# A graph network's last sweep: block sums accumulated in seven PSUM banks, gathered rows already multiplied by the neighbour weights

## The chip, the cores and the metric

The kernel runs on one core of a Trainium2 chip. The metric is the time of one execution on the device in microseconds (us), the median of several runs. Engines: PE (TensorE, matmuls; PEld are its weight loads), DVE (VectorE), ACT (ScalarE), POOL (GpSimd), SP (SyncE, which here issues DMAs and passes signals on).

## What is computed

12500 nodes with 64 features x, 200000 edges (src, dst) sorted by dst, a vector of 64 per edge. Two layers:

```
h1  = relu(layernorm(x) ...)                        layer 1: attention (GATv2, 4 heads) over
x1  = x + gatv2(h1, src, dst, edge_attr)            the edges of each node, softmax per node
h2  = relu(layernorm(x1) ...)
out = x1 + mean_over_edges_into_n(h2[src]) @ w_l.T + h2 @ w_r.T + b      layer 2
```

The last line is the last sweep: for each node the mean of the rows h2[src] of its edges, times a 64x64 matrix, plus a product of its own row.

## The kernel before, in words

Nodes are cut into 98 blocks of 128, edges into 1563 tiles of 128. Since edges are sorted by dst, the tiles of a block are neighbours; a **slot** is one pair of tile and block (a tile on the border of two blocks has two), padded to 1664, and four slots make a **quad**, so there are 416. The first two stages (up to about 4125 us) sort out layer 1; the columns and lines on them play no part here. Between them and the last sweep the rows h2 are made on DVE in four quarters of the blocks and stored by SP to h2D in DRAM (`stored_rows`, L1312 to L1318).

Then comes a prologue: DVE clears the sums AG (128x6272 in SBUF, L1339) and adds b to X3 (L1352), and PE, ACT and DVE make each pair of blocks' own product: transpose (L1357), copy (L1359), matmul by V_r (L1367), addition to X3 (L1370). Names: BR, ZR, AL, mS, mR, sm are SBUF areas, PS is PSUM, and C is the constant identity.

In the last sweep each engine runs a loop of its own over the quads, and they meet by semaphores:

- POOL (`gathers3`, L1417): one indirect DMA per tile brings its 128 rows h2[src] into a ring of 128 tiles (32 quads) in SBUF. Before each quad it takes one from `gf`, which starts at 7: POOL is at most 7 quads of tiles ahead of DVE's quads of slots (there are more slots than tiles, so the distance grows).
- SP (`landings3`, L1394) turns the landing of a quad into an increment of `landed3`.
- PE (`sums3`, L1441): per slot one matmul of a 128x128 one-hot matrix (which edge goes to which node) by 128 gathered rows, start and stop in one, into one of four PSUM banks (q % 4). It waits for the one-hots (`o3_rdy`, in the order listings p3_1) and for `landed3`; its fourth matmul of a quad increments `a3_rdy` (p3_2).
- DVE (`adds3`): per quad it waits for `a3_rdy`, gives `gf` its increment (L1457), and adds the four 128x64 results into AG (L1460); behind the first of them it makes the one-hots of the quad two further on (`onehots`, L544). `c3_acc` (p3_3) chains the additions.
- ACT (`tables3`, L1379) copies the next column of dst numbers to mR.

Where a matmul reads and an addition writes is loaded into registers from tables (`Table`, L528), for PE from DRAM.

```
                a3_rdy.take(V)
                V.sem_inc(gf.s, 1)
                for k in range(4):
                    c3_acc.take(V)
                    V.tensor_tensor(to[k], to[k], bank3(q)[:, k, :], ALU.add).then_inc(c3_acc.s, 1)
                    if k == 0:
                        onehots(q + 2).then_inc(o3_rdy.s, 1)
```

After a barrier the last phase takes each pair of blocks of AG: transpose (L1484), copy (L1488), matmul by V_l (L1496), times 1/count plus X3 (L1502); SP stores seven pieces of out (L153).

Of the kernel before, what the change touches and what calls it, by code (L numbers as in the profile page):

```python
# [4 lines left out]
NB = 98  # L5
NP = NB * 128
NT = 1563
NS = 1664
# [12 lines left out]
def build(nc, x, src_t, dst_t, dfirst, ea, w_l, b_l, w_r, b_r, w_e, rep, bias, v_l, v_r, cst, trow, out):  # L21
# [67 lines left out]
    h2D = dram("h2D", [NP, F])  # L89
# [4 lines left out]
    tabD = dram("tabD", [3, NS], i32)  # L94
    NQ1 = NS // 4
# [1122 lines left out]
    gf, o3_rdy, a3_rdy, c3_acc, go3, r3f, r3_rdy = flows("p3_", 7)  # L1218
    i3 = flows("i3_", 4)
    S.sem_inc(gf.s, 7)  # L1220
    S.sem_inc(c3_acc.s, 1)
# [7 lines left out]
    bT3 = rbf_[0:1, NS:2 * NS].bitcast(i32)  # L1229
    dma(S, bT3, tabD[0:1, :], dB)  # L1230
# [49 lines left out]
    dH2, h2v = dsem(), h2D.rearrange("(b p) f -> p b f", p=128)  # L1280
# [3 lines left out]
    there = [0] * 4  # L1284

# [26 lines left out]
    def stored_rows(k):  # L1312
# [4 lines left out]
        sv.wait(S)  # L1317
        dma(S, h2v[:, b], H23[:, b], dH2)  # L1318

    normalised_nodes(0)  # L1320
# [7 lines left out]
    stored_rows(0)  # L1328
    variance(1)
    centred(3)  # L1330
    stored_rows(1)
    variance(2)
    variance(3)
    stored_rows(2)
    stored_rows(3)
    sv.wait(Q)
    v(V.tensor_copy(b1_ps, b1))
    v(V.tensor_copy(iota_ps, iota))
    v(V.memset(AG, 0.0))  # L1339
    dB.wait(V)  # L1340
    sg.wait(V)
    dH2.wait(Q)

    sa.wait(A)
    for half in range(4):
        A.copy(mS[:, half, :], sT[:, 16 * half:16 * half + 16]).then_inc(i3[half].s, 16)
        A.copy(mR[:, half, :], rel3[:, 16 * half:16 * half + 16]).then_inc(r3_rdy.s, 1)

    at = {}
    sv.wait(P)  # L1350
    dW.wait(P)
    v(V.tensor_tensor(X3, X3, bc(b1_ps.unsqueeze(1), [128, NB, F]), ALU.add))  # L1352
    for p in range(NB // 2 + 1):
        if p < NB // 2:
            if p >= 2:
                P.wait_ge(sa.s, at["copy", p - 2])
            sp.on(P.transpose(PS[:, p % 2, 0:128], H2[:, 128 * p:128 * p + 128], ident))  # L1357
            sp.wait(A)
            sa.on(A.copy(z4[:, p % 4, :], PS[:, p % 2, 0:128]))  # L1359
            at["copy", p] = sa.n  # L1360
        if p >= 1:
            p -= 1
            P.wait_ge(sa.s, at["copy", p])
            if p >= 4:
                P.wait_ge(sv.s, at["own", p - 4])
            m = PS[:, 2 + p % 4, 0:128].rearrange("p (t f) -> p t f", f=F)
            sp.on(P.matmul(PS[:, 2 + p % 4, 0:128], z4[:, p % 4, :], W3[:, 1, :, :].rearrange("p t f -> p (t f)"),  # L1367
                           start=True, stop=True))
            sp.wait(V)
            sv.on(V.tensor_tensor(X3[:, 2 * p:2 * p + 2, :], X3[:, 2 * p:2 * p + 2, :], m, ALU.add))  # L1370
            at["own", p] = sv.n
    sv.wait(P)

    def tables3():

        with A.Fori(0, NS // 64 - 1) as i:
            for half in range(4):
                r3f.take(A)
                A.copy(mR[:, half, :], rel3[:, ds(i * 64 + 64 + 16 * half, 16)]).then_inc(r3_rdy.s, 1)  # L1379
            close(r3f)  # L1380
        r3f.take(A)
        A.copy(mR[:, 0, :], rel3[:, 0:16]).then_inc(r3_rdy.s, 1)

    landed3, seen = nc.alloc_semaphore("landed3"), Flow("seen")
    S.sem_inc(seen.s, 4)
# [18 lines left out]
    def gathers3():  # L1404

        def some(n):
            for j in range(n):
# [9 lines left out]
                Q.indirect_dma_start(BIG[:, j * F:j * F + F], None, h2D,  # L1417
# [4 lines left out]
        with Q.Fori(0, NG3 // G):  # L1422
            some(G)
        some(NG3 % G)

    def bank3(q):
        return PS[:, q % 4, 0:4 * F].rearrange("p (s f) -> p s f", f=F)

    need = [P.alloc_register(f"nd{q}") for q in range(16)]

    def sums3():

        with P.Fori(0, NS // 64) as i:
            pt = Table(P, tabD[2:3, :], i, "sl", (G - 1) * F, 64)
            P.load(need, needD[0:1, ds(i * 16, 16)])
            for j in range(64):
# [5 lines left out]
                if j % 4 == 3:  # L1442
                    ins.then_inc(a3_rdy.s, 1)
# [99 lines left out]
```

## Time and profile before

| | |
|---|---|
| three runs | 6836.62, 6867.18, 6873.22 us; median 6867.18 |
| span of the profiled execution, first to last instruction | 6810.8 us (the page gives no further time of this execution) |
| busy: PE, DVE, ACT, POOL | 4219.0, 3344.2, 1439.7, 3619.4 us |
| first and last gather of the last sweep | 4417.0 and 6701.6 us |
| moved by DMA | 478 MB, 70 GB/s over the span |

The page divides the span into busy time of each engine and slices; groups of instructions stand by line, with the idle time of the engine just before them and what ended it ("<-remote" is a signal whose sender the trace doesn't name, "<-issue" is no wait at all). Queues that only issue or signal have a q behind the engine's name (DVEq, SPq).

### The profile page before, as it was taken

The page shows a single profiled execution, that of the slowest core. Times are in us where ns is not written, and L with a number is a line of the kernel's source. Part 1 is how long each engine was busy: PE and PEld are TensorE (multiplying, and loading weights), DVE is VectorE, ACT ScalarE, POOL GpSimd, SP SyncE. Part 2 cuts the span into 40 slices and gives each one's busy share as a digit, 9 for nine tenths or more (in the row PEclk, how much of TensorE's full clock was granted, in tenths as well). Part 3 has the DMA queues.
Part 4 walks back from the last instruction along what each step waited for, and adds up shares of the span by engine and source line. Part 5 has one row for each costly group of instructions (what it writes and reads, how often), then busy time and mean ns, then how long its engine had stood idle before and what let it go on. Part 6 is the DMA issues. An engine that isn't in the chain of part 4 may idle for free. (4 is left out here: it accounts for less than half of the span.)

```text
span 6810.8 us, 81310 instructions
## 1 busy us (share of the span) xinstructions
PE 4219.0 (62%) x16760; PEld 3105.7 (46%) x16761; DVE 3344.2 (49%) x8382; ACT 1439.7 (21%) x6145; POOL 3619.4 (53%) x3589
## 2 busy tenths in 40 slices
PE   4777777777777777768999998533333333333335
PEld 3555555555555555644444445333333333333335
DVE  6444444444444444479999998822222222222224
ACT  1111111111111111236666663400000000000000
POOL 2555555555555555305555551056666666666662
PEclk8888888888888888879999998755555555555555
DMA  6333333333333333324343441201111111111111
GB/s 106 92 93 95 93 93 94 95 99 95 96 93 93 98 92 93 98 81 124 110 111 109 110 112 50 57 20 23 23 23 23 23 23 23 23 23 23 23 23 28
DMA packets 609795, 478.35 MB, mean 70 GB/s; under 512 B 424696, under 2 KB 438034, under 8 KB 609334
## 3 DMA queue, kind: packets, MB, share of 16 engines
q1 hardware_dynamic: 440940, 256.05, 14.3%
q0 software_dynamic: 101184, 104.41, 7.2%
q10 hardware_dynamic: 67465, 115.81, 4.7%
q14 instruction: 158, 1.29, 0.1%
q8 instruction: 48, 0.79, 0.0%
HBM read 348.37 MB, written 126.73 MB: 70 GB/s over the span
## 5 line engine op out<-in xcount | busy, mean ns | idle before, releaser
L1417 POOL DMA_INDIRECT BR<-h2D,mS x1564 | 1476.9, 944 | 1007.4 <-issue 451.5
L585 POOL DMA_INDIRECT BR<-hD,AL x1308 | 1247.2, 953 | 1018.4 <-ACT ZR L634 638.4
L1441 PE MATMUL PS<-BR,ZR 128*128 x3328 | 796.1, 426 | 1507.1 <-DVE ZR L544 1086.3
L616 PE MATMUL PS<-Wz,BR 128*128 128x264 f32 x3328 | 1209.0, 449 | 696.3 <-DVE alq L682 319.0
L1441 PEld LDWEIGHTS PS<-BR,ZR 128*128 128x128 f32 x3328 | 735.9, 328 | 1567.3 <-issue 1563.9
L679 DVE SCALAR_TENSOR_TENSOR PS<-PS,a 128x528 f32<-128x528 f32 x832 | 594.8, 715 | 1543.4 <-PE PS L617 653.6
L1460 DVE TENSOR_TENSOR BR<-BR,PS 128x64 f32 x1664 | 362.6, 218 | 1725.3 <-remote 1306.5
L617 PE MATMUL PS<-BR 128*128 x3328 | 1150.8, 431 | 0.0
L940 PE MATMUL PS<-BR,ZR 128*128 128x329 f32 x3328 | 1027.9, 469 | 27.0 <-POOL BR L926 21.0
L616 PEld LDWEIGHTS PS<-Wz,BR 128*128 128x128 f32 x3328 | 653.9, 219 | 839.0 <-issue 587.1
L926 POOL TENSOR_TENSOR BR<-ZR,BR 128x768 f32<-128x768 f32 x416 | 616.1, 1481 | 416.6 <-ACT BR L912 414.7
L954 DVE TENSOR_TENSOR BR<-BR,PS 128x329 f32 x1664 | 812.4, 488 | 20.3 <-PE PS L940 13.2
L617 PEld LDWEIGHTS PS<-BR 128*128 128x128 f32 x3328 | 728.3, 219 | 155.0
L940 PEld LDWEIGHTS PS<-BR,ZR 128*128 128x128 f32 x3328 | 501.4, 188 | 553.3 <-DVE ZR L864 521.1
L642 ACT COPY BR<-PS 128x256 f32<-128x256 f32 x832 | 309.2, 372 | 1917.3 <-PE PS L603 862.0
L682 DVE TENSOR_REDUCE alq<-PS 128x8 f32<-128x528 f32 x832 | 578.3, 698 | 0.0
L1379 ACT COPY mR<-ZR 128x16 f32 x100 | 20.4, 204 | 2243.8 <-issue 1163.6
L864 DVE TENSOR_TENSOR ZR<-PS,mR 128x128 f32<-128x128 f32 x1676 | 473.7, 283 | 2.2 <-PEq L161 2.2
L915 ACT ACTIVATE BR<-ZR,BR 128x64 f32<-128x64 f32 x1664 | 440.8, 336 | 0.0
L634 ACT COPY ZR<-BR 128x64 f32 x1664 | 326.5, 247 | 355.9 <-issue 190.3
L585 POOL DMA_INDIRECT BR<-hD,lmS x256 | 243.4, 951 | 280.6 <-ACT ZR L634 170.7
L603 PE MATMUL PS<-C,ZR 128*128 128x128 f32 x1664 | 342.3, 293 | 69.7 <-ACT ZR L634 44.9
(254 smaller groups left out, 2641.4 us busy)
## 6 DMA issues: line engine op xcount, KB each, us to landing
zD<-ZR ACTq DMA_DIRECT2D x416, 256.0 KB
ZR<-zD SPq DMA_DIRECT2D x416, 256.0 KB, 2.7
BR<-relD SPq DMA_DIRECT2D x105, 512.0 KB
ZR<-ea SPq DMA_DIRECT2D x1664, 32.0 KB
BR<-h2D,mS POOLq DMA_INDIRECT x1564
BR<-hD,AL POOLq DMA_INDIRECT x1308
AL<-hD SPq DMA_DIRECT2D x28, 224.0 KB, 2.6
BR<-hD,lmS POOLq DMA_INDIRECT x256
```

The lines of the kernel that those rows point to most:

```text
L585: Q.indirect_dma_start(HT[:, (t % G) * F:(t % G) * F + F], None, hD, bass.IndirectOffsetOnAxis(at_src, 0)).then_inc(hs[q % 16], 16)
L616: P.matmul(m, zo1[:, p % 2, (j % 2) * 128:(j % 2) * 128 + 128], Wz, start=True, stop=False)
L617: ins = P.matmul(m, ohT[:, (j // 4) % 2, j % 4, :], xr, start=False, stop=True)
L679: return V.scalar_tensor_tensor(m, m, 0.0, bc(a8.unsqueeze(1), [128, 2, MC]), ALU.max, ALU.mult)
L682: return V.tensor_reduce(alq[:, (p // 8) % 2, 8 * (p % 8):8 * (p % 8) + 8].rearrange("p (s h) -> p s h", h=H), scores_of(p).rearrange("p s ...
L864: return V.tensor_tensor(oh[:, (s // 4) % 4, s % 4, :], iota_ps, bc(mR[:, (s // 16) % 4, s % 16:s % 16 + 1], [128, 128]), ALU.is_equal)
L915: ins = A.activation(r[:, n, 192:256], hb[:, k, n, 0, :], ACT.Copy, scale=r[:, n, 259:260])
L926: Q.tensor_tensor(r[:, :, 0:192].rearrange("p s (h f) -> p s h f", f=F), bc(hb[:, q % 4, :, 0, :].unsqueeze(2), [128, 4, 3, F]), bc(r[:, : ...
L940: P.matmul(PS[:, j % 7, 0:AC], oh[:, (j // 4) % 4, j % 4, :], rows2(j // 4)[:, j % 4, :], start=True, stop=True).then_inc(ag_rdy.s, 1)
L954: V.tensor_tensor(a, a, PS[:, j % 7, 0:AC], ALU.add).then_inc(c2_acc.s, 1)
L1417: Q.indirect_dma_start(BIG[:, j * F:j * F + F], None, h2D, bass.IndirectOffsetOnAxis(mS[:, (j // 16) % 4, j % 16:j % 16 + 1], 0)).then_inc ...
L1441: ins = P.matmul(bank3(j // 4)[:, j % 4, :], oh[:, (j // 4) % 4, j % 4, :], rows, start=True, stop=True)
```

## The change

- The rows in DRAM are now g2 = h2 times V_l (`neighbour_rows`): PE transposes a quarter's pairs of blocks in groups of four, ACT copies them to `turned2`, PE multiplies by V_l, ACT copies to YC, and SP stores to g2D. The quarters are 32, 24, 24 and 18 blocks. `turned2` also serves the own products, now 49 matmuls with 13 additions of 128x512.
- PE's matmuls of the sweep accumulate (start and stop False) directly where the block's sum stands: block b in bank (b // 8) % 7. No addition on DVE and no AG.
- ACT (`flush3`): when the slots of eight blocks are through (`placed`), it copies them out, times 1/count, and clears the bank (`flushed`). DVE adds each group of eight to X3 after its one-hots; ACT stores out in pieces of 16 blocks, and the last two blocks go by DVE and SP. The last phase with transposes and matmuls is gone.
- Three increments leave PE per quad: `placed` (to ACT), `gf` (to POOL, no longer by way of DVE), `oh_free` (to DVE, p3_3 in the order listings after).
- Ring of 256 tiles (64 quads), window `gf` of 38 quads, one-hots 16 quads ahead.
- PE waits for `landed3` once in eight slots and for `flushed` once in 16; its tables come from SBUF. Twelve small DVE operations and three small DMAs make the tables.

```diff
-    S.sem_inc(gf.s, 7)
-    S.sem_inc(c3_acc.s, 1)
+    landed3, flushed, placed = (nc.alloc_semaphore(n) for n in ("landed3", "flushed", "placed"))
+    S.sem_inc(gf.s, 38)
+    S.sem_inc(seen.s, 4)
+    S.sem_inc(oh_free.s, 16)
+    S.sem_inc(flushed, 1)
...
-    quarters = [slice(0, 25), slice(25, 49), slice(49, 74), slice(74, NB)]
+    quarters = [slice(0, 32), slice(32, 56), slice(56, 80), slice(80, NB)]
...
+    def neighbour_rows(k):
...
+        def turn(p, n, g):
+            if g >= 2:
+                P.wait_ge(sa.s, at["kept", g - 2])
+            for t in range(n):
+                ins = P.transpose(PS[:, g % 2, 128 * t:128 * t + 128], H2[:, 128 * (p + t):128 * (p + t) + 128], ident)
+            sp.on(ins)
+            sp.wait(A)
+            sa.on(A.copy(turned2[:, 128 * p:128 * (p + n)], PS[:, g % 2, 0:128 * n]))
+            at["kept", g] = sa.n
+
+        def product(p, n, g):
+            P.wait_ge(sa.s, at["kept", g])
...
+            for t in range(n):
+                ins = P.matmul(PS[:, 4 + g % 2, 128 * t:128 * t + 128], turned2[:, 128 * (p + t):128 * (p + t) + 128], V_l,
+                               start=True, stop=True)
+            sp.on(ins)
+            sp.wait(A)
+            sa.on(A.copy(YC[:, 128 * p:128 * (p + n)], PS[:, 4 + g % 2, 0:128 * n]))
...
+        sa.wait(S)
+        dma(S, g2v[:, quarters[k]], YC3[:, quarters[k]], dG2)
...
-    v(V.memset(AG, 0.0))
...
+    RING, ONES, BANKS = 256, 16, 7
+    oh3 = BIG[:, 16384:16384 + ONES * 512].rearrange("p (q s n) -> p q s n", q=ONES, n=128)
...
+    v(V.memset(PS[:, 0:BANKS, :].rearrange("p k c -> p (k c)"), 0.0))
...
-                Q.indirect_dma_start(BIG[:, j * F:j * F + F], None, h2D,
+                Q.indirect_dma_start(BIG[:, j * F:j * F + F], None, g2D,
...
         with P.Fori(0, NS // 64) as i:
-            pt = Table(P, tabD[2:3, :], i, "sl", (G - 1) * F, 64)
-            P.load(need, needD[0:1, ds(i * 16, 16)])
+            row = Table(P, rows_of, i, "sl", (RING - 1) * F, 64)
+            to = Table(P, sums_at, i, "pb", (8 * BANKS - 1) * F, 64)
+            P.load(gate[0:8], need_at[0:1, ds(i * 8, 8)])
+            P.load(gate[8:12], spill_at[0:1, ds(i * 4, 4)])
             for j in range(64):
-                rows = ahead(P, BIG[:, ds(pt(j), F)])
+                if j % 16 == 0:
+                    P.wait_ge(flushed, P.snap(gate[8 + j // 16], min_val=1, max_val=15 - BANKS))
+                rows, sums = ahead(P, BIG[:, ds(row(j), F)]), ahead(P, SUMP[:, ds(to(j), F)])
                 if j % 4 == 0:
                     o3_rdy.take(P)
-                    P.wait_ge(landed3, P.snap(need[j // 4], min_val=1, max_val=NG3 // 4))
-                ins = P.matmul(bank3(j // 4)[:, j % 4, :], oh[:, (j // 4) % 4, j % 4, :], rows, start=True, stop=True)
+                if j % 8 == 0:
+                    P.wait_ge(landed3, P.snap(gate[j // 8], min_val=1, max_val=NG3 // 4))
+                ins = P.matmul(sums, oh3[:, (j // 4) % ONES, j % 4, :], rows, start=False, stop=False,
+                               skip_group_check=True)
+                if j % 4 == 0:
+                    ins.then_inc(placed, 1)
+                if j % 4 == 1:
+                    ins.then_inc(gf.s, 1)
                 if j % 4 == 3:
-                    ins.then_inc(a3_rdy.s, 1)
+                    ins.then_inc(oh_free.s, 1)
...
+            for q in range(16):
+                oh_free.take(V)
+                V.tensor_tensor(oh3[:, q % ONES, :, :], bc(iota_ps.unsqueeze(1), [128, 4, 128]),
+                                bc(rel3[:, ds(i * 64 + 4 * q, 4)].unsqueeze(2), [128, 4, 128]), ALU.is_equal
+                                ).then_inc(o3_rdy.s, 1)
...
+    def flush3(g):
+
+        A.wait_ge(placed, A.snap(ends_r[g], min_val=1, max_val=NS // 4))
+        for u in range(8):
+            b = 8 * g + u
+            ins = A.activation(SUMS[:, b * F:b * F + F], PS[:, g % BANKS, u * F:u * F + F], ACT.Copy, scale=rc[:, b:b + 1])
+        sa.on(ins)
+        sa.wait(A)
+        A.activation(PS[:, g % BANKS, :], nothing, ACT.Copy, scale=0.0).then_inc(flushed, 1)
...
+    def added3(g):
+
+        V.wait_ge(flushed, g + 2)
+        sv.on(V.tensor_tensor(X[:, 512 * g:512 * g + 512], X[:, 512 * g:512 * g + 512], SUMS[:, 512 * g:512 * g + 512], ALU.add))
```

DVE where the sweep begins; before (AG's additions, PS the four banks, BR the sums):

```order
L1452 UNCONDITIONAL_BRANCH [waits p3_6]
L1452 ISA
L528 TENSOR_LOAD BR
L529 ISA
L533 ISA x2
L533 REGISTER_ALU
L1460 TENSOR_TENSOR BR<-BR,PS 128x64 [waits p3_2,p3_3]
L544 TENSOR_TENSOR ZR<-PS,mR 128x512
L1460 TENSOR_TENSOR BR<-BR,PS 128x64 [waits p3_3] x3
```

and after (L1455 clears the seven banks, L1529 is the loop's start):

```order
L1452 TENSOR_TENSOR AL<-AL,PS 128x128 [waits sp]
L1455 MEMSET PS 128x3584 [waits sv]
L1529 UNCONDITIONAL_BRANCH [waits d23,sv]
L1532 ISA [waits p3_3]
L1532 TENSOR_TENSOR BR<-PS,ZR 128x512
```

The four additions with their chain are out of the loop, and what is left per quad is a wait for `oh_free` and one 128x512 operation. DVE behind its loop, after:

```order
L1532 ISA [waits p3_3]
L1532 TENSOR_TENSOR BR<-PS,ZR 128x512
L1529 REGISTER_ALU [waits p3_3]
L1529 COMPARE_AND_BRANCH
L1561 TENSOR_TENSOR AL<-AL,BR 128x512 [waits flushed] x12
L1581 SCALAR_TENSOR_TENSOR AL<-PS,rc,AL 128x64 [waits p3_3]
L1581 SCALAR_TENSOR_TENSOR AL<-PS,rc,AL 128x64
```

Twelve additions of eight blocks stand behind all one-hots, and each waits for ACT's flush; in the kernel before the loop was followed by a barrier and 98 L1502.

PE where the sweep begins; before:

```order
L1433 UNCONDITIONAL_BRANCH [waits sv]
L1435 TENSOR_LOAD needD_ptr
L1435 ISA
L1435 REGISTER_ALU
L1435 TENSOR_LOAD needD
L528 TENSOR_LOAD tabD_ptr
L528 ISA
L528 REGISTER_ALU
L528 TENSOR_LOAD tabD
L529 ISA
L1441 MATMUL PS<-BR,ZR 128x64 [waits p3_1,landed3]
L529 ISA
```

and after (the loads from ZR at L1507 and L1508 are the two gates, L529 the two tables):

```order
L1504 UNCONDITIONAL_BRANCH [waits d26,sv]
L1504 ISA
L1507 TENSOR_LOAD ZR
L1508 ISA
L1508 TENSOR_LOAD ZR
L529 ISA [waits flushed]
L529 TENSOR_LOAD BR
L530 ISA
L529 TENSOR_LOAD ZR
L530 ISA
L1517 MATMUL PS<-BR 128x64 [waits p3_1,landed3]
L530 ISA
```

The loads from DRAM have become loads from SBUF, one more table is read, a wait for `flushed` has come in ahead, and the matmul has no bank of its own.

## Rows read from the trace of the kernel before

**Rows 1.** The page's first line.

```profile
span 6810.8 us, 81310 instructions
```

**Rows 2.** Busy time by stretch: us, busy (xcount) of PE, PEld, DVE, ACT, POOL; PEclk; DMA share; GB/s.

```profile
4417.00:4452.00 35.00, 11.97 (x45) 8.89 (x45) 9.38 (x14) 3.70 (x15) 26.56 (x28) 0.60 0.11 26
...
4484.00:6702.00 2218.00, 739.69 (x3087) 682.52 (x3086) 536.46 (x1927) 19.57 (x96) 1449.64 (x1536) 0.50 0.11 23
6702.00:6781.00 79.00, 54.49 (x234) 51.23 (x234) 42.28 (x153) 1.02 (x5) 0.58 (x1) 0.50 0.01 1
6781.00:6811.00 30.00, 26.05 (x146) 19.03 (x145) 23.29 (x98) 12.99 (x49) 0.00 (x0) 0.90 0.48 108
```

**Rows 3.** The gathers (L1417): durations in ns; idle time ended by, us and times.

```profile
L1417 POOL DMA_INDIRECT BR<-h2D,mS x1564: 939/945/1062, 4417.0 to 6701.6; - x196
...
  issue: 451.5, 1482
  DVEq L1457: 357.3, 81
```

**Rows 4.** Waits in 4480 to 6811: waiting operation, releaser: us, times, longest.

```profile
DVE BR L1460 <- remote: 1306.5, 132, 16.7
```

**Rows 5.** Groups of instructions in 4480 to 6811: busy us, mean ns, idle before.

```profile
L1441 PE MATMUL PS<-BR,ZR 128*128 x3328 | 796.1, 426 | 1507.1 <-DVE ZR L544 1086.3 <-issue 411.3
...
L1460 DVE TENSOR_TENSOR BR<-BR,PS 128x64 f32 x1664 | 362.6, 218 | 1725.3 <-remote 1306.5 <-issue 198.7 <-PE PS L1441 122.5
L544 DVE TENSOR_TENSOR ZR<-PS,mR 128x512 f32<-128x512 f32 x416 | 284.3, 684 | 0.2 <-issue 0.2
```

**Rows 6.** The same view, 6702.7 to 6781.

```profile
L544 DVE TENSOR_TENSOR ZR<-PS,mR 128x512 f32<-128x512 f32 x30 | 20.5, 684 | 0.0
```

**Rows 7.** Timeline, middle of the last sweep: start, duration, operation, idle before it.

```profile
5601.13 3.67 PE L1441 MATMUL PS<-BR,ZR 128*128 x16 [2.09 <-issue]
...
5608.86 1.96 PE L1441 MATMUL PS<-BR,ZR 128*128 x8 [4.06 <-DVE ZR L544]
...
5617.94 0.94 POOL L1417 DMA_INDIRECT BR<-h2D,mS  x1 [0.30 <-issue]
5622.88 0.22 DVE L1460 TENSOR_TENSOR BR<-BR,PS 128x64 f32 x1 [13.52 <-remote]
...
5623.56 0.94 POOL L1417 DMA_INDIRECT BR<-h2D,mS  x1 [4.67 <-DVEq L1457]
...
5639.32 0.22 DVE L1460 TENSOR_TENSOR BR<-BR,PS 128x64 f32 x1 [7.38 <-remote]
```

**Rows 8.** The additions of the stage before (L954), idle time ended by.

```profile
  PE PS L940: 13.2, 21
```

**Rows 9.** Register loads of a table from SBUF on PE (first stage).

```profile
L528 PEldq TENSOR_LOAD <-sm x104: 1102/1107/1297, 165.3 to 2961.4; - x104
```

**Rows 10.** Waits in 4415 to 4484, as rows 4.

```profile
ACT BR L1359 <- remote: 25.2, 6, 6.8
```

**Rows 11.** Timeline before and at the start of the gathers, as rows 7.

```profile
4390.80 1.82 DVE L1316 SCALAR_TENSOR_TENSOR BR<-BR,sm 128x1600 f32<-128x1600 f32 x1
...
4407.19 1.76 DVE L1316 SCALAR_TENSOR_TENSOR BR<-BR,sm 128x1536 f32<-128x1536 f32 x1
...
4416.97 1.06 POOL L1417 DMA_INDIRECT BR<-h2D,mS  x1 [198.67 <-DVE BR L1339]
...
4417.67 0.42 PE L1357 MATMUL PS<-C,BR 128*128 128x128 f32 x1
...
4418.31 0.42 PE L1357 MATMUL PS<-C,BR 128*128 128x128 f32 x1
```

**Rows 12.** Timelines of the end, and landing time of the stores (L153).

```profile
6706.11 3.48 PEld L1441 LDWEIGHTS PS<-BR,ZR 128*128 128x128 f32 x16 [2.25 <-SPq L1394]
...
6807.75 0.37 SPq L153 DMA_DIRECT2D out<-AL  x1
...
DMA to landing us min/median/max: 3.0/3.0/3.5
```

More of the change, by code:

```diff
@@ L94, in build @@
     tabD = dram("tabD", [3, NS], i32)
+    tab3D = dram("tab3D", [3, NS], i32)
     NQ1 = NS // 4
@@ L1228, in build @@
             dma(S, W3[64 * t:64 * t + 64, w, t, :], frm, dW)
-    bT3 = rbf_[0:1, NS:2 * NS].bitcast(i32)
-    dma(S, bT3, tabD[0:1, :], dB)
+    from3 = sm[:, 11, 0:26].rearrange("p (t k) -> p t k", t=2).bitcast(i32)
+    with nc.allow_non_contiguous_dma(reason="two small tables, once"):
+        for t in range(2):
+            dma(S, from3[:, t, :], tabD[t, :].rearrange("(k p) -> p k", p=128), dB)
     dma(S, X3, x.rearrange("(b p) f -> p b f", p=128), dX)
@@ L1372, in build @@
[L1372 to L1385, printed above, removed]
+    RING, ONES, BANKS = 256, 16, 7
+    oh3 = BIG[:, 16384:16384 + ONES * 512].rearrange("p (q s n) -> p q s n", q=ONES, n=128)
@@ new lines, in build @@
+    v(V.tensor_copy(grp, to3[:, 2, :]))
+    v(V.tensor_scalar(grp, grp, float(2 - BANKS), 1.0, ALU.add, ALU.max))
+    v(V.tensor_copy(to3[:, 2, :], grp))
+    sv.wait(A)
+    with nc.allow_non_contiguous_dma(reason="three small tables, once"):
+        for t in range(3):
+            dma(A, tab3D[t, :].rearrange("(k p) -> p k", p=128), to3[:, t, :], dT3)
+    v(V.tensor_tensor(below3, bc(blk.unsqueeze(1), [128, 12, 13]), bc(iota[:, 8:104:8].unsqueeze(2), [128, 12, 13]), ALU.is_lt))
+    sv.wait(P)
@@ new lines, in build @@
+    sp.on(P.matmul(PS[:, 6, 0:156], allone, below3.rearrange("p g k -> p (g k)"), start=True, stop=True))
+    sp.wait(V)
+    v(V.tensor_reduce(ends, PS[:, 6, 0:156].rearrange("p (g k) -> p g k", k=13), AX.X, ALU.add))
+    v(V.tensor_scalar(ends, ends, 6.0, None, ALU.add))
+    v(V.tensor_copy(ends_i, ends))
+    v(V.tensor_scalar(ends_i, ends_i, 2, None, ALU.arith_shift_right))
+    sums_end = sv.n
+    dT3.wait(A)
+    dTL = dsem()
+    dma(A, rows_of, tab3D[0:1, :], dTL)
+    dma(A, sums_at, tab3D[1:2, :], dTL)
@@ new lines, in build @@
+    with nc.allow_non_contiguous_dma(reason="each eighth and each sixteenth entry of two small tables"):
+        dma(A, need_at, needD[0:1, 1:NQ1:2], dTL)
+        dma(A, spill_at, tab3D[2:3, 15:NS:16], dTL)
+    v(V.tensor_copy(b1_ps, b1))
+    v(V.tensor_copy(iota_ps, iota))
+    v(V.tensor_tensor(X3, X3, bc(b1_ps.unsqueeze(1), [128, NB, F]), ALU.add))
+    P.wait_ge(sa.s, at["stored", group[0] - 1])
+    for g in range(13):
+        p, n = 4 * g, min(4, NB // 2 - 4 * g)
+        if g >= 6:
+            P.wait_ge(sv.s, at["own", g - 6])
+        for t in range(n):
+            ins = P.matmul(PS[:, g % 6, 128 * t:128 * t + 128], turned2[:, 128 * (p + t):128 * (p + t) + 128], V_r,
+                           start=True, stop=True)
+        sp.on(ins)
+        sp.wait(V)
+        sv.on(V.tensor_tensor(X[:, 128 * p:128 * (p + n)], X[:, 128 * p:128 * (p + n)], PS[:, g % 6, 0:128 * n], ALU.add))
+        at["own", g] = sv.n
@@ L1387, in landings3 @@
+    sv.wait(V)
+    v(V.memset(PS[:, 0:BANKS, :].rearrange("p k c -> p (k c)"), 0.0))
+    sv.wait(P, A)
+    dTL.wait(P)
+    dR.wait(V)
     def landings3():
```

176 lines of the change are left out of this document (82 added, 94 removed).

## The prediction

> **What bounds the kernel now.** I read the page first for its slices, then the windows of the stretches, then the last sweep's gathers, its waits and its groups, and last the timeline of one stretch in it. The span is 6810.8 us [rows 1]; the page gives no time beside it, and the median of the three runs is 6867.2, 56.4 more. I sum against the span and add 56.4 at the end. A difference of 0.5% (34 us) is about the least that a measurement of this kernel can tell from no change.
>
> In the last sweep (4484 to 6702) POOL is busy 1450 of 2218 us, PE 740, DVE 536, and the DMA engines 11% [rows 2]: no engine is full. The gathers run from 4417.0 to 6701.6, and POOL stood 357.3 us in 81 waits for DVE's signal from L1457 [rows 3]; one of these is the 32 us between the 28th gather and the 29th. All others are alike: 20 gathers back to back, start to start 1.249 us (0.945 busy and 451.5 / 1482 = 0.304 of issue), then 4.1 us of pause ((357.3 - 32.1) / 80). DVE and PE in turn wait for each other: DVE 1306.5 us in 132 waits, the longest 16.7, at the first addition of a quad [rows 4].
>
> Is the data late? No: once the last gather is out, 30 quads' one-hots are still to come [rows 6], in the 79 us up to the last phase [rows 2], a quad in 2.5 us. So POOL is then some 32 quads ahead of DVE, the whole ring, and had the data been late there would be no such queue. What is late is the word from PE to DVE. In the timeline PE ends eight records (one quad) at 5610.82, DVE has nothing else to do, and its next addition starts at 5622.88, after 13.52 us of idleness, 4 us after POOL stopped; then POOL gets its signal and goes on [rows 7]. This recurs with each pause: increments from PE's matmuls to DVE are held while POOL issues gathers back to back, and come when it rests. In the stage before, with no gathers, DVE waited for the same kind of increment only 13.2 us in all, 21 times [rows 8]. I can't say what holds them. So the sweep is a loop: window full, POOL stops, the held increments come, DVE signals, POOL runs 20 gathers. It takes 2298 us for 416 quads, 5.52 each, where POOL's own work would be 4 x 1.25 = 5.0.
>
> **The change, part by part.**
>
> Gathers. The window is 38 quads instead of 7, the ring 64 quads instead of 32, and POOL's signal comes from PE's second matmul of a quad directly, no longer through DVE. A held increment must now be overdue by 38 quads (190 us) rather than by seven before POOL feels it, and the holds seen are up to 16.7 us. I take the pauses as gone: 1563 intervals of 1.249 us are 1952 us, against 2285 from first to last start now. Gather size and source layout are as before, so I keep these durations.
>
> One-hots. DVE makes them 16 quads ahead instead of two, and no longer adds (1664 additions, 363 us [rows 5], and their three chained waits a quad are gone). Per quad DVE has 0.68 us [rows 5] in 5.0; a hold of 17 us is 3.4 quads of the 16. Hidden.
>
> PE. The same 1664 matmuls of two passes, 796 us in all or 1.9 a quad [rows 5], at 1.2 GHz (granted 0.50 [rows 2]). The register loads are ten per 64 slots and all from SBUF, 1.107 us each [rows 9]. So 16 x 1.9 + 10 x 1.1 = 42 us in 80 per 64 slots. Hidden; a clock of 0.50 costs nothing as long as POOL sets the pace. Three increments leave per quad instead of one: one to ACT, one to POOL, one to DVE. The trace of before doesn't show three; bounds are nothing and 5.52 us for each (rival D). I take nothing. The nearest rows are of 4415 to 4484, where PE, ACT and DVE pass increments to and fro for each of 49 pairs, most of them beside gathers: ACT idled for late ones six times, 6.8 us at the longest [rows 10], and such a wait is far shorter than the reserve of each of the three receivers.
> By the Trainium skill ("TensorE: Matmul & The Clock Gate", the section on the per-tile semaphore tail) increments are written one after another, about 26.3 ns each, and one on the last matmul should do. By that, 832 more would be an estimated 22 us on PE, hidden as well, and no increment would take microseconds; the 13.52 us of [rows 7] are against that rule as a full account.
>
> ACT. Per eight blocks it waits, copies eight 128x64 out of PSUM (under 0.5 us each, by the 0.68 that DVE takes for 128x512 [rows 5]) and clears a bank: 5 us in some 160. PE's wait for a cleared bank comes seven banks later. Hidden. The 12 additions of 128x512 (0.68 each) come on DVE in the last 80 us, when its one-hots are done; the 12th waits for block 95, 32 tiles (40 us) before the end; the stores are issued on ACT behind these. All hidden, the last excepted.
>
> Before the sweep. Rows of products need PE, two ACT copies and a store from YC. A transpose and a two-pass product take 0.64 us a pair of blocks here (start to start of transposes [rows 11]); 49 pairs are 31 us at 1.2 GHz and half of that at 2.4. The first quarter's rows, now ready at 4392.6 (4390.80 + 1.82), come about 1.5 us later with 32 blocks in place of 25, the last at 4408.95 as now: the quarters are cut anew, the elements are the same [rows 11]. Fast, PE is done 4 us after the last; slow, at 4425 to 4427. From the last rows (4407.19 + 1.76) to the first gather it is 8.0 us [rows 11], mostly the store; kept, with 0.5 for a copy. First gather between 4421.5 and 4435.5; in 4417 to 4452, with the same kind of work, the clock was 0.60, so between the levels [rows 2]; I take 4426: **+9**. The own products (49 matmuls and 13 additions, no transposes), the addition of b to X3, the 12 small table operations and the clearing of seven banks end at about 4450, beside the first 152 gathers, which need no signal and last until 4616. Hidden, even at three times the length.
>
> The end. Now 109.2 us from the start of the last gather to the span's end: 79 of queued quads and 30 of the last phase [rows 2, 3]. After: no queue, since PE keeps up and follows each landing: 4.5 us from the last gather to its quad's first weights (an upper bound: 6706.11, after a wait for a landing [rows 12], less 6701.6), two quads of 2.1, two short DVE operations (0.6), issue 0.37 and landing 3.0 [rows 12]: 12.7 us.
>
> **Sum.** 4426 + 1952.2 = 6378.2 for the last gather (now 6701.6, -323.4), + 12.7 = span 6390.9 (-419.9), + 56.4 = **6447 us**.
>
> **Rivals.**
>
> B. One-hots run out. POOL never rests, so perhaps DVE's increments come only at a pause. PE would use up 16 quads and stop, until POOL fills its window: (1564 - 152) / 64 = 22 pauses of 4.1 us, +90: **6537**. For: the hold of [rows 7] ends with POOL's pause. Against: in the next stretches of the same timeline others ended while POOL ran (7.38 us of idleness up to 5639.32, with gathers on both sides [rows 7]).
>
> C. The loop stays, whatever the window: holds hit PE, ACT and POOL's signal alike, so that beyond the first window each 20 gathers still cost 28.9 us. 190 + 1412 x 1.445 = 2230, last gather at 6656, then up to 60 queued quads at 2.1 and 10 of end: span 6792, **6848**, no change. Against: nothing in the new window ties a pause to 20 gathers.
>
> D. Slower: each of the three increments is paid for by itself. If a matmul that carries one cannot be followed before it is delivered, and delivery under gathers takes the 5.52 us of a present quad with its one increment, 3 x 416 = 1248 of them are 6889 us instead of 2298: about **11460**. It decides from 1.88 us per increment ((6810.8 - 4450 - 8) / 1248). For: 832 new increments in exactly the place where increments are slow. Against: PE runs 16 records without a gap over a quad's end [rows 7], so it doesn't wait for its own. This is also where the skill's advice on one increment points, with a far larger price than it states.
>
> E. The change doesn't do what it says, or a wait I haven't seen (a bank not cleared, a gate of landings only once in eight slots) costs a few per cent.
>
> **How the numbers follow.** Forecast as summed 0.72; B 0.13; C 0.08; D 0.04; E 0.03, taken as faster. Faster by over 0.5%: 0.72 + 0.13 + 0.03 = 0.88; within 0.5%: C, 0.08; slower: D, 0.04. The range begins at 6410 (first gather 4.5 us earlier, and the lowest run, 30.6 below the median) and goes to 6560, which takes in B with the late first gather (+9.5) and part of E; it leaves out C and D.
>
> **What would show it.** In the changed profile: gathers start at 4421 to 4436; 1563 starts 1.25 us apart, POOL's wait for PE's signal near zero; the last gather near 6378 and 13 us behind it; PE waits for landings, not for DVE, in the sweep; DVE's idle time is large and harmless. B shows as pauses of POOL each 64 gathers and PE waiting for one-hots; C as pauses each 20; D as gaps in PE's records behind each third of the matmuls. Wrong would be: a cadence other than 1.25 (gathers beside ACT's and PE's new work), a first gather later than 4440, or a tail of over 30 us.

## The result: half a per cent, not six

The changed kernel took 6828.1 us (median of 12 runs, 6805.5 to 6854.7), the kernel before 6866.0 (12 runs); ratio 0.9949, 95% interval 0.993 to 0.9969. That is 38 us less, where 420 were forecast. The profiled execution took 6817.4 us of its own with a span of 6816.0, so what lies around a span is 1.4 us. The 56.4 that I had added to the span of before were therefore no overhead: 55 of them are the difference between the profiled execution of before and the median of the three runs.

One thing has to be said here because nothing below can be read without it. The experiments were run in several jobs, and these met two kinds of execution. In **kind A** the kernel before takes 6837 to 6891 us; this is the kind of both kernels' times above and of the profile that the prediction was made from. In **kind B** it takes 5534 to 5546 us. All kernels of a job are of one kind. Each job with experiments ran on another chip of the machine (kind A on chips 2, 0 and 6, kind B on 5 and 4), so it can't be told whether the kind belongs to the chip or to the moment. Where kernels are compared below, they are of the same kind, and most rows below are of a single execution.

The profile after (kind A), first line and stretches of the sweep; columns as in [rows 2]:

```profile
span 6816.0 us, 76889 instructions
```

```profile
4540.00:4720.00 180.00, 17.20 (x65) 18.38 (x64) 5.53 (x8) 0.00 (x0) 136.04 (x144) 0.50 0.12 27
4720.00:6704.00 1984.00, 656.98 (x2744) 648.33 (x2745) 229.41 (x343) 23.44 (x90) 1303.70 (x1380) 0.50 0.11 23
6704.00:6816.00 112.00, 101.52 (x468) 100.22 (x467) 39.81 (x61) 4.69 (x18) 0.94 (x1) 0.50 0.13 29
```

In the first of these stretches the wide window is not yet used up, and POOL issues 144 gathers without a pause. In the same 180 us PE starts 65 matmul passes, that is 32 slots (two passes each), where the gathers bring 144 tiles. After the last gather PE is busy 102 of 112 us with what has piled up. The gathers, as [rows 3]:

```profile
L1490 POOL DMA_INDIRECT BR<-g2D,mS x1564: 938/944/1390, 4490.3 to 6704.2; - x196
...
  issue: 454.6, 1484
  remote: 260.5, 71
```

The first comes at 4490.3 and the last at 6704.2: 2213.9 us instead of 2284.7 [rows 3], and POOL still waits 260.5 us, now for `gf` from PE (17.6 us more stand under PE by name). The tail behind the last gather is 111.8 us, where it was 109.2. The waits of the sweep (4440 to 6816), as [rows 4]:

```profile
DVE BR L1532 <- remote: 1548.1, 160, 22.4
PEld PS L1517 <- issue: 1525.4, 900, 17.0
PE PS L1517 <- issue: 1505.4, 876, 16.8
ACT BR L1546 <- remote: 1371.7, 7, 207.1
```

PE is idle 1505 us in 876 pieces, and the profile names nothing for it ("issue"). For one-hots it waited 23.3 us in the whole sweep, for landings 5.0. The timeline shows what these pieces are:

```profile
4600.17 0.29 PEld L1517 LDWEIGHTS PS<-BR 128*128 128x128 f32 x1 [1.13 <-issue]
4600.22 0.94 POOL L1490 DMA_INDIRECT BR<-g2D,mS  x1 [0.30 <-issue]
4601.47 0.95 POOL L1490 DMA_INDIRECT BR<-g2D,mS  x1 [0.30 <-issue]
4601.55 0.27 PE L1517 MATMUL PS<-BR 128*128 x1 [1.82 <-issue]
4602.73 0.94 POOL L1490 DMA_INDIRECT BR<-g2D,mS  x1 [0.30 <-issue]
4602.95 0.29 PEld L1517 LDWEIGHTS PS<-BR 128*128 128x128 f32 x1 [2.50 <-issue]
...
4604.35 0.26 PE L1517 MATMUL PS<-BR 128*128 x1 [2.54 <-issue]
...
4605.75 0.29 PEld L1517 LDWEIGHTS PS<-BR 128*128 128x128 f32 x1 [2.51 <-issue]
```

Weight loads and matmuls start 1.4 us apart, where [rows 7] has eight of each in 1.96. In the stretch up to 4720 a slot takes 180 / 32.5 = 5.5 us on the mean. I call such a stretch a spell. Later most spells last some 20 to 50 us each and end at once. Here one ends, 15 passes follow back to back, and DVE gets three quads together:

```profile
5631.87 0.27 PE L1517 MATMUL PS<-BR 128*128 x1 [1.15 <-issue]
5632.57 0.29 PEld L1517 LDWEIGHTS PS<-BR 128*128 128x128 f32 x1 [1.13 <-issue]
5633.97 3.27 PE L1517 MATMUL PS<-BR 128*128 x15 [1.83 <-issue]
5633.98 3.28 PEld L1517 LDWEIGHTS PS<-BR 128*128 128x128 f32 x15 [1.12 <-issue]
5634.16 1.89 DVE L1532 TENSOR_TENSOR BR<-PS,ZR 128x512 f32<-128x512 f32 x3 [4.31 <-remote]
5634.23 0.94 POOL L1490 DMA_INDIRECT BR<-g2D,mS  x1 [2.51 <-remote]
```

So it was not only the word from PE to DVE that came late in the kernel before; PE itself is slowed. With room for 38 quads it falls behind by some 32 quads until 4720, and when the last gather is out 468 passes, 58 quads of slots, are still to come.

### The profile page after: what moved, and what is told of

Same layout as the page of the kernel before. It is cut to its first block and busy times, and to the rows that moved or that the text cites. A ratio compares the mean times of both kernels' runs of the same rounds, so it can differ in the third digit from the quotient of the medians.

```text
span 6816.0 us, 76889 instructions
## 1 busy us (share of the span) xinstructions
PE 4216.2 (62%) x16713; PEld 3144.7 (46%) x16714; DVE 3025.9 (44%) x6612; ACT 1436.5 (21%) x6076; POOL 3614.7 (53%) x3589
## 5 line engine op out<-in xcount | busy, mean ns | idle before, releaser
L1490 POOL DMA_INDIRECT BR<-g2D,mS x1564 | 1478.5, 945 | 954.0 <-issue 454.6
L1517 PE MATMUL PS<-BR 128*128 x3328 | 788.8, 388 | 1532.1 <-issue 1505.4
L1517 PEld LDWEIGHTS PS<-BR 128*128 128x128 f32 x3328 | 778.9, 320 | 1542.0 <-issue 1525.4
L1532 DVE TENSOR_TENSOR BR<-PS,ZR 128x512 f32<-128x512 f32 x416 | 278.0, 689 | 2009.5 <-remote 1548.1
L618 PE MATMUL PS<-BR 128*128 x3328 | 1154.8, 433 | 0.0
L618 PEld LDWEIGHTS PS<-BR 128*128 128x128 f32 x3328 | 729.3, 219 | 156.6
L941 PEld LDWEIGHTS PS<-BR,ZR 128*128 128x128 f32 x3328 | 503.3, 189 | 552.4 <-DVE ZR L865 517.9
L1546 ACT ACTIVATE BR<-PS,rc 128x64 f32<-128x64 f32 x96 | 20.9, 329 | 2297.2 <-remote 1371.7
L604 PEld LDWEIGHTS PS<-C,ZR 128*128 128x128 f32 x1664 | 242.3, 154 | 379.1 <-ACT ZR L635 218.8
```

The source lines that it names most:

```text
L604: ins = P.transpose(PS[:, p % 2, (j % 2) * 128:(j % 2) * 128 + 128], zring[:, j % 32, :, :].rearrange("p t f -> p (t f)"), ident)
L618: ins = P.matmul(m, ohT[:, (j // 4) % 2, j % 4, :], xr, start=False, stop=True)
L941: P.matmul(PS[:, j % 7, 0:AC], oh[:, (j // 4) % 4, j % 4, :], rows2(j // 4)[:, j % 4, :], start=True, stop=True).then_inc(ag_rdy.s, 1)
L1490: Q.indirect_dma_start(BIG[:, j * F:j * F + F], None, g2D, bass.IndirectOffsetOnAxis(mS[:, (j // 16) % 4, j % 16:j % 16 + 1], 0)).then_inc ...
L1517: ins = P.matmul(sums, oh3[:, (j // 4) % ONES, j % 4, :], rows, start=False, stop=False, skip_group_check=True)
```

## The experiments

The theories. (A **pass** is one weight load with its matmul; an fp32 slot has two.) **Increments**: each increment that PE sends under gathers is paid for. **Steps**: whatever PE issues in a spell takes 0.7 us or a multiple, so what counts is how much it issues. **Passes**: each pass that PE makes under gathers is slow, so half as many would let it keep up. **Ring**: PE is held by reading what gathers write. A fifth came up on the way, **rest**: the gathers themselves can't be kept up at 1.249 us, and PE's spells are only where this shows.

All kernels here pass each register that a semaphore is waited against through one more operation, the maximum with 1. Two are nothing but that:

> The changed kernel; the values that semaphores are waited against in registers pass one more register operation (maximum with 1) on ACT and PE, nothing else. Both theories: last sweep as in the profile of the change, first to last gather 2214 us, POOL pausing some 280 us in all. It also shows how far the stages before the sweep scatter: in the profile of the change the first of them ended 52 us later than in that of before (3140 against 3088), though its code is the same. If that is scatter of an execution, it lies anywhere between 3080 and 3145 here; if it belongs to the change, it is 3140 again.

> The kernel before with the same extra register operation. First to last gather 2285 us, 80 pauses of 4.1 us. If the place where the first stage ends (3088) is a matter of the single execution, it differs here by some 10 to 50 us.

Kind A. The change: 6855.5 us, gathers from 4527.9 to 6743.9 (2216.1), tail 110.2. Before: 6847.8 us, 4465.5 to 6734.3 (2268.8), tail 112.2. So the sweep repeats within 1%, and the stages ahead of it don't: the first stage's last gather came at 2831 and 2878 in the two executions of before, at 2884 and 2924 in those of the change. The last is later than either of my guesses for it allowed (the stage behind it began at 3180, not by 3145). That scatter of 50 us is larger than the effect, and I count from the first gather of the sweep from here on.

**Increments, passes.** One increment per quad. The window's start value is 22 here, because DVE passes 16 more on at once, so the distance is 38 quads as before:

```diff
-                if j % 4 == 0:
-                    ins.then_inc(placed, 1)
-                if j % 4 == 1:
-                    ins.then_inc(gf.s, 1)
...
                 oh_free.take(V)
+                V.sem_inc(gf.s, 1)
+                V.sem_inc(placed, 1)
```

> The changed kernel with one increment per quad on PE instead of three; DVE passes on the two others (to POOL and ACT) when it takes the first. Theory 'increments' (each increment that leaves PE under gathers is paid for): with a third of them first to last gather falls from 2214 to POOL's own 1952 us or near it, time down by some 250. Theory 'passes' (under back-to-back gathers every pass of PE, with or without an increment, completes only each 0.7 to 2.8 us): no gain, first to last gather 2190 to 2240.

2222.2 us (kind A), tail 115.8, 6839.5 us: no gain. "Increments" falls, and my rival D with it.

```diff
-    oh3 = BIG[:, 16384:16384 + ONES * 512].rearrange("p (q s n) -> p q s n", q=ONES, n=128)
+    oh3 = BIG[:, 16384:16384 + ONES * 256].bitcast(bf16).rearrange("p (q s n) -> p q s n", q=ONES, n=128)
...
-                ins = P.matmul(sums, oh3[:, (j // 4) % ONES, j % 4, :], rows, start=False, stop=False,
+                ins = P.matmul(sums, oh3[:, (j // 4) % ONES, j % 4, :], rows.bitcast(bf16).rearrange("p (f t) -> p f t", t=2)[:, :, 1], start=False, stop=False,
```

> The changed kernel with bf16 one-hots and only the upper half (bf16) of each gathered float read by the matmul, so one pass (one weight load, one matmul) per slot instead of two; increments, waits and gathers are as in the change. It leaves out the lower 16 bits of the gathered rows. Theory 'passes': PE has half as many to complete and keeps up; first to last gather near 1952, pauses of POOL under 50 us, the queue behind the last gather short, time some 6550 or less. Theory 'increments': the three per quad are still there, first to last gather 2190 to 2240, no gain.

2313.0 us (kind A), tail 136.6, 6943.6 us: slower, with half the passes. So "passes" falls too. The bf16 slice needs more register operations for its address (3.4 FUSED_REGOPS, ALU operations and MOVEs per slot instead of 1.4), and these stretch too. The register operations of one line on PE's queue, with the shortest, median and longest duration in ns:

```profile
L532 PEldq FUSED_REGOPS  x3328: 1/53/1398, 157.7 to 6939.6; - x196
L532 PEldq MOVE  x1664: 1/29/1398, 4510.9 to 6939.5; - x185
```

A MOVE between registers reads no ring and writes no PSUM, and it takes up to 1.4 us. This is against "ring", and it is what "steps" was drawn from.

**No register operations, fixed addresses.**

```diff
-                rows, sums = ahead(P, BIG[:, ds(row(j), F)]), ahead(P, SUMP[:, ds(to(j), F)])
+                rows, sums = BIG[:, 24576 + F * (j % 8):24576 + F * (j % 8) + F], PS[:, 6, F * (j % 4):F * (j % 4) + F]
```

> The changed kernel, but PE's matmuls of the sweep have fixed addresses: rows from eight places that no gather writes, sums into one bank that ACT leaves alone, so the sums aren't those of the edges. No register operation or table load is left per slot on PE; passes (two weight loads, two matmuls a slot), increments and waits stay. Theory 'instruction steps' (while POOL gathers back to back, PE's sequencer needs 0.7 or 1.4 us for each thing that it issues, register operations as much as passes: in the run with bf16 rows register operations on PE took 700 ns where they take 140): four things a slot instead of five or so, first to last gather falls from 2216 to 2100 to 2200. Rival 'ring' (a pass waits because gathers write the ring that it reads): PE is fast, 1952 and a short tail.

> The same with bf16 operands, so one weight load and one matmul per slot and nothing else on PE; sums are again not those of the edges. Instruction steps: two things a slot where the bf16 run had five or six; at 1.1 to 1.4 us each 2.5 us a slot, 10 a quad in the slow spells, still above POOL's 5.0, but half of the fp32 case: first to last gather 1952 to 2080. Were only register operations slow: 1952.

Both fell into kind B: 1951.2 and 1951.5 us, tails of 9.5 and 6.4, 5524.3 and 5524.4 us, beside 5545.7 for before. They say nothing on the spells, since there are none in this kind. The repeat was of kind B too (1951.7 us):

> Fixed addresses on PE (as a_static; sums are not those of the edges). Quick kind: as before, 1951 us from first to last gather. Slow kind: with no register operations on PE, 4 things a slot instead of five; 'instruction steps' says 2050 to 2200, 'ring' says 1952.

The third was of kind A:

> Fixed addresses on PE in the last sweep, no register operations (sums are not those of the edges). If before takes some 6870 us here (spells occur): 'instruction steps' says four things a slot instead of five, first to last gather 2050 to 2200, spells still there; 'ring' (PE held by reading what gathers write) says 1952. If before takes some 5540: 1952 by both, nothing learnt.

2226.3 us, tail 105.4, 6778.9 us. Neither the register operations nor the reading of the ring is worth anything: "ring", which gave 1952, falls, and "steps", which gave 2050 to 2200, is missed as well.

**The two kernels in kind B.**

> The changed kernel once more, timed beside before. In the second job the kernel before took 5545.7 us where it had taken 6837 to 6891, and PE kept up with back-to-back gathers without a slow spell. If this execution is of the quick kind (before near 5550): first to last gather 1952 us, no pause, tail some 13 us, ratio to before 0.995 to 0.998 (before's own cadence then is 1.249 too and only its last phase and queue differ). If it is of the slow kind (before near 6870): as the first profile, 2214 and 112.

> The kernel before once more. Quick kind: its gathers too run at 1.249 with no 4 us pauses, 1952 us from first to last, and the end after the last gather is 30 us of last phase and a few us of queue, 35 to 45 in all. Slow kind: 2269 to 2285 and 109 to 112 us behind.

The change: 5522.4 us (9 runs), before 5538.9 (12), ratio 0.9972, interval 0.9962 to 0.9982. Gathers of the change, and of the kernel before:

```profile
L1493 POOL DMA_INDIRECT BR<-g2D,mS x1564: 940/945/1420, 3565.6 to 5519.3; - x196
its engine sat idle before it (us, times) until:
  issue: 473.2, 1553
```

```profile
L1420 POOL DMA_INDIRECT BR<-h2D,mS x1564: 940/944/1061, 3540.5 to 5495.4; - x196
its engine sat idle before it (us, times) until:
  issue: 471.4, 1547
  DVE BR L1342: 199.0, 1
  DVEq L1461: 4.4, 2
```

1953.6 and 1954.9 us. In kind B the kernel before has no pauses either, with its window of 7 quads; it waits for DVE 4.4 us in all. What is left of the change is the end, 9.5 us for 40.3, less 25.1 us that the first gather is later; 7.9 of these are scatter of the stages ahead. The end of the change:

```profile
5519.25 0.94 POOL L1493 DMA_INDIRECT BR<-g2D,mS  x1 [0.30 <-issue]
5522.84 3.49 PEld L1522 LDWEIGHTS PS<-BR 128*128 128x128 f32 x16 [2.68 <-SPq L1470]
5522.84 3.67 PE L1522 MATMUL PS<-BR 128*128 x16 [2.49 <-SPq L1470]
5526.56 0.48 DVE L1587 SCALAR_TENSOR_TENSOR AL<-PS,rc,AL 128x64 f32<-128x64 f32 x2 [25.98 <-PE PS L1522]
5527.06 0.39 SPq L154 DMA_DIRECT2D out<-AL  x1
```

**No gathers.**

```diff
-                Q.indirect_dma_start(BIG[:, j * F:j * F + F], None, g2D,
-                                     bass.IndirectOffsetOnAxis(mS[:, (j // 16) % 4, j % 16:j % 16 + 1], 0)
-                                     ).then_inc(g1[q % 16], 16)
+                Q.memset(BIG[:, j * F:j * F + F], 1.0).then_inc(g1[q % 16], 16)
+                pc.take(Q)
+                Q.memset(BIG[:, 24576:25088], 0.0).then_inc(pc.s, 1)
```

> The changed kernel without the gathers of the last sweep: POOL fills each ring place with a 128x64 memset and then clears 128x512, about the same busy time, and raises the same semaphores; sums are not those of the edges. If it is the gathers (their descriptors and packets) that slow PE, PE runs at its 1.9 us a quad and POOL sets the pace with no wait for PE. If POOL's mere business does it, PE has the same slow spells and POOL pauses.

> No gathers in the last sweep, memsets of like length on POOL instead (sums are not those of the edges). If spells occur and the gathers cause them: the sweep runs at POOL's 0.68 us a tile or PE's 1.9 us a quad, 930 to 1000 us, no register operation over 0.5 us on PE in it, while the first stage, which keeps its gathers, is as slow as in the first profiles (last gather of it at about 2880). If POOL's business causes them: the sweep takes 1200 us or more.

The first fell into kind B (sweep 925 us, 4491.8 us in all), the second into kind A; its sweep in columns as in [rows 2]:

```profile
4452.00:5377.00 925.00, 743.55 (x3328) 717.87 (x3327) 298.99 (x434) 28.13 (x108) 908.78 (x3125) 0.50 0.03 5
```

Again 925 us, with POOL busy 98% and PE 80%, while the first stage, which keeps its gathers, took as long as ever in this kind (its last one at 2.84 ms against 2.09). The two kinds are the same where nothing is gathered: the stage in between ([rows 8] are of it) has its additions start from 3088.0 to 4125.6 in the profile of before and from 2210.0 to 3248.1 in kind B, 1038 us each. The gathers make the difference, and not POOL's business.

**Rest between gathers.**

```diff
                                      ).then_inc(g1[q % 16], 16)
+                pc.take(Q)
+                Q.memset(BIG[:, 24576:24592], 0.0).then_inc(pc.s, 1)
```

> The changed kernel with a 128x16 memset on POOL behind each gather (some 0.15 to 0.2 us), so a cadence of about 1.45 us: 1563 gathers last 2270 us at least. If only an unbroken stream of gathers slows PE, it now keeps up: no pauses on POOL beyond these, tail behind the last gather 112 us down to 15, time as before or 50 less. If gathers slow PE whatever their spacing, the pauses stay on top: first to last gather 2450 or more.

Kind B: the memset fills the 0.30 us of issue and the cadence is 1.267; 1978.9 us, tail 9.5. My expectation of 1.45 was wrong. The repeat, of kind B as well, gave 1980.8, tail 9.5:

> The memset behind each gather. Quick kind: first to last gather 1979 as in the last job, since the memset fits into the 0.30 us of issue. Slow kind: if slow spells need an unbroken stream, 2000 to 2100 and a short tail; if not, 2214 or more.

The third was of kind A:

> A 128x16 memset between gathers (cadence 1.267 instead of 1.249, and a semaphore round on POOL). If spells occur: should a rest in the stream end them, first to last gather 1980 and a short tail; if they go by the number of gathers, 2214 as in the change.

2244.4 us, tail 103.8, 6802.8 us: a cadence of 1.267 is still too dense. With 400 columns instead of 16:

> A memset of 128x400 behind each gather, 0.42 us, so an even cadence of about 1.55 us: 1563 of them last 2420 us. If spells occur and end by rests of POOL in any form: no waits of POOL for PE, PE at most a few quads behind, tail under 30 us. If a spell, once begun, needs one long rest, PE lags by tens of quads as in the change and the waits come on top. Where before takes 5540: 2420 and a short tail.

Kind A: 2457.0 us, cadence 1.57, tail 9.5, 6975.5 us. The sweep's gathers and PE in it:

```profile
L1494 POOL DMA_INDIRECT BR<-g2D,mS x1564: 949/950/1322, 4507.7 to 6964.7; - x196
its engine sat idle before it (us, times) until:
  issue: 271.3, 1556
```

```profile
L1525 PE MATMUL PS<-BR 128*128 x3328 | 764.4, 424 | 1696.6 <-SPq L1471 1667.4 <-issue 29.3
```

POOL has no wait for PE, and PE waits for landings alone (SPq L1471): "issue" is 29 us, where it was 1505. But for the table loads, which take 1.1 us in kind B too, not one register operation on PE's queue was over 0.5 us. In kind A too PE is untouched when a gather is started only every 1.57 us. (I had expected 1.55 and 2420 us.)

**Little work on PE, small window.** First a quarter of the matmuls:

```diff
+                if j % 4 != 3:
+                    continue
                 ins = P.matmul(sums, oh3[:, (j // 4) % ONES, j % 4, :], rows, start=False, stop=False,
```

> The changed kernel with one matmul per quad instead of four on PE (fixed addresses, the one increment of a quad on it, DVE passes on the others; the sums are not those of the edges). If spells occur: should their length go by what PE has to issue, a quarter of it keeps up and first to last gather is 1952 to 1990; should POOL's rest be what the sweep needs, whatever PE does, it stays at 2200 to 2240. Where before takes 5540: 1952 by both.

Kind A: 2164.1 us, tail 47.9, 6737.1 us. This is below the 2200 to 2240 that I gave for "rest", but far above the 1952 to 1990 of the other theory. PE keeps up well enough for POOL never to wait for it. But the gathers are slower all the same:

```profile
L1493 POOL DMA_INDIRECT BR<-g2D,mS x1564 | 1658.6, 1060 | 724.6 <-issue 506.1 <-DVE AL L1455 218.2 <-DVEq L1535 0.3
```

A gather now takes 1060 ns in the mean (943 to 952 in the other runs) and the gaps 0.32: 1.385 us each. This is the row that settles most. Take POOL's waits away, and POOL itself is stretched. It is not so from the start, though. Of three stretches of 200 us, with POOL's busy time and gathers, TensorE's granted clock, DMA share and GB/s, the first is at full pace and the others are not:

```profile
4524.00:4724.00 200.00, 151.26 (x161) 0.51 0.19 27
4800.00:5000.00 200.00, 154.33 (x143) 0.50 0.13 24
6400.00:6600.00 200.00, 152.54 (x144) 0.50 0.13 24
```

Counted by the start times, the first 179 gathers here, and the first 180 in the profile of the change, follow each other at 1.25 us in the mean without a pause. Only behind them does the sweep come down to 1.40 and 1.44 us a gather.

Then the small window:

```diff
-    S.sem_inc(gf.s, 38)
+    S.sem_inc(gf.s, 7)
```

> The changed kernel with the window of before, 7 quads instead of 38, all else as in the change. If spells occur: 2260 to 2290 from first to last gather as in before, if the window is what gave the 70 us; 2216 if the rest of the change gave them. Where before takes 5540: 1952, since PE keeps within 7 quads.

Kind A: 2219.2 us, tail 55.7, 6772.3 us. The window is worth nothing for the gathers, and the wide one costs some 55 us at the end: beside the 6873.0 of the kernel before in the same job, this is the better form of the change (one execution of each).

| kind A | first to last gather | per gather | behind it |
|---|---|---|---|
| before, two executions | 2284.7, 2268.8 | 1.462, 1.452 | 109.2, 112.2 |
| change, two executions | 2213.9, 2216.1 | 1.416, 1.418 | 111.8, 110.2 |
| one increment | 2222.2 | 1.422 | 115.8 |
| bf16 rows | 2313.0 | 1.480 | 136.6 |
| fixed addresses | 2226.3 | 1.424 | 105.4 |
| 128x16 memset | 2244.4 | 1.436 | 103.8 |
| window 7 | 2219.2 | 1.420 | 55.7 |
| a quarter of PE's matmuls | 2164.1 | 1.385 | 47.9 |
| 128x400 memset | 2457.0 | 1.572 | 9.5 |

Issued at 1.249 or 1.267 us, a gather costs 1.385 to 1.48 in kind A over the whole sweep, and spells on PE or longer gathers on POOL make up the difference; at 1.57 nothing is stretched. What the other engines issue seems to move this within 7%: the figure is least with a quarter of the matmuls and most with the added register operations of the bf16 rows. So in kind A the sweep can't keep up more than about one gather in 1.4 us, and that is the bound of both kernels. "Rest" is the one of the five theories that no run contradicts, though it put the quarter of the matmuls some 40 us too high. What it is that fills up isn't shown. It is not the gathers' own data transfer: the DMA engines are busy 11 to 13% in either kind, and by the packets in the traces a gather's 32 packets are through 2.0 us after its start at the median, in the profile of the change as in kind B.

**A rival that no run tests: the recording.** Each gather raises its landing semaphore by 16, so the sweep has 25024 such increments. Of their records the traces of kind B hold 25016 or more. Those of kind A hold 3617 for the change, 3957 for the kernel before, 2420 with a quarter of the matmuls, but 23689 with the 128x400 memset. Without gathers nothing is missing: in the sweep's 925 us the two memset runs have 7713 (B) and 7708 (A) records of increments of all kinds. (These are counts in the packed traces.) This fits the many "remote" waits of kind A. The wait below is of the change in kind B and names PE; in kind A it stands as `DVE BR L1532 <- remote` in the waits above:

```profile
DVE BR L1537 <- PE PS L1522: 1594.1, 400, 8.2
```

So records are lost in kind A exactly where gathers are dense and the engines slow. The timed executions of the changed kernel each have a span and a granted clock on record, so something was recorded in all of them, and what the kernels take without any recording is not known. The recording may be what can't keep up, with spells and pauses as its price, or both may come from a third thing.

## Why the prediction was wrong

**The step that failed** is "I take the pauses as gone: 1563 intervals of 1.249 us are 1952 us". I had read the pauses as the window's, since each follows 20 gathers and ends with DVE's signal [rows 3, 7]. They were what dense gathers had to pay in this kind of execution, so (357.3 - 32.1) us of pauses turned into 260.5 us of waits for PE. With the window of 7 the change's gathers take 2219.2 us, with that of 38 2213.9 and 2216.1: the window was never what held them. The term measured 2213.9 us, 262 more than forecast. In kind B the same term is 1953.6, right within 0.1%; but there the kernel before has it too.

- **"PE. Hidden"** failed in kind A with it: 42 us of work per 80 was right for PE's own rate, but in spells a quad takes 22 us. The line "no queue, since PE keeps up" follows, and the tail was 111.8 instead of 12.7. In kind B it was 9.5.
- **Word late or engine slow.** I had "increments are held" from [rows 4, 7]. The trace of before could not tell that from a slowed PE, because four banks let PE run at most a few quads ahead. The comparison with the stage without gathers [rows 8] was right and pointed at the cause: gathers. I drew the wrong bound from it. That POOL's back-to-back stretches in the trace in the sweep were never longer than 28 gathers should have been the warning: nothing in it showed 1.249 us sustained. Even the 180 gathers without a pause that open the profile of the change would have been too short a sample.
- **First gather: +9.** This term was too small. It was +25.1 in kind B: 7.9 from ahead of it, 3.3 in the layer norm's chain, and 22.0 instead of 8.0 from the last rows on. PE and ACT took 9.0 of these (4467.7 to 4476.7), inside my 4 to 17. The last store took 12.3 us for 576 KB, where before 5.9 did for 768 KB:

```profile
g2D<-BR SPq DMA_DIRECT2D x1, 576.0 KB, 12.3
BR<-g2D,mS POOLq DMA_INDIRECT x4
tab3D<-sm ACTq DMA_DIRECT2D x3, 6.5 KB
```

  Beside it run the three small tables of 6.5 KB each, 5040 packets together (landing after 20 us in kind B), issued 0.2 us behind it and ahead of the first gather. I had given them no term. That they are what slows the store is my reading; no run leaves them out.
- **Increments at nothing** was right: one or three per quad, 2222.2 and 2216.1 us. The Trainium skill's figure ("TensorE: Matmul & The Clock Gate", "The cost: per-tile semaphore tail", 26.3 ns each) is compatible with that, since by it 832 more increments are an estimated 22 us, which PE's 1505 us of idle time would hide, and it doesn't explain the spells.
- **One-hots, ACT, DVE's additions, own products** were hidden as said, in both kinds.
- **Rivals.** C had the right outcome (the loop stays whatever the window, 6848 against 6828) and I gave it 0.08, with "nothing in the new window ties a pause to 20 gathers" against it. The loop that stayed isn't C's, though: the pauses are 71 and not one to each 20 gathers, so C's number is near by luck. B's pauses and D's price per increment didn't occur. D's 11460 has the 56.4 in it twice (4450 + 6889 + 8 + 56.4 = 11403).

The sum as it is, kind A, means of two executions from the first gather to the end: gathers -62, tail +0, so -62. The first gather is 17 later by the change itself (25.1 of kind B less the 7.9 of scatter): -45, beside the -38 of the medians; the stages ahead scatter by more than what is left. Why the change's gathers cost 1.417 and those of before 1.457 isn't settled; the window isn't it, nor are the increments.

## What to carry to other kernels

A pause that a profile puts down to a wait may be the payment for a rate that can't be sustained. Before a gain is counted from closing such gaps, find a stretch in the trace where the engine ran without them for as long as it would have to; here the longest was 28 gathers out of 1564, and even 180 were sustained where 1564 were not. A wider window only helps if the consumer is faster on average, and otherwise it moves the wait to the end: with 7 quads instead of 38 the tail was 55.7 us and not 110. Where a trace has many "remote" waits, count whether its records of increments are complete, before the slow stretches are put down to the kernel.

## What the runs showed of the hardware

- The same kernel takes 5539 or 6866 us, by the job it is run in. Stretches without gathers are equal (1038 us, and 925 for the sweep with memsets), those with gathers aren't: 2.09 against 2.83 to 2.92 ms up to the first stage's last gather, 1955 against 2269 to 2285 in the last sweep of the kernel before. What tells the kinds apart is open; records of increments are complete in the one and up to nine tenths of the gathers' are missing in the other.
- In kind A PE's queue issues in steps of 0.7 us during a spell, moves between registers included (up to 1.4 us, against 0.03 at the median), and SP's queue has single register operations of the same length.
- An indirect gather of 128 rows of 256 bytes takes 0.944 us on POOL, but 1.060 in the mean in the run where POOL waited for nothing (a quarter of the matmuls, kind A).
